# A two-layer sequence kernel on one core: the second sequence's norm scaling moved from VectorE to ScalarE, and a prefetch hint on TensorE's loop

## The chip, the cores and the metric

The kernel runs on one core of one Trainium2 chip. The metric is the device time of one execution in microseconds (us), lower is better. The kernel before was run three times: 1784.64 us is the median, 1784.25 and 1787.32 us are the lowest and the highest.

## What is computed

Sixteen sequences of 256 tokens and 512 features pass through two layers. Only the norms matter for the change:

```python
# layer 0: layer norm with gain and shift from the condition, latent attention with a
# sparse mask (16 heads of 32), then the residual
x = x + attention0(h) @ Wo.T
# layer 1: two RMS norms, each with a gain from the condition
def ada_rms(x, t, w, tw):
    n = x * jax.lax.rsqrt(jnp.mean(jnp.square(x), axis=-1, keepdims=True) + EPS)
    scale = t @ tw.T
    return n * (w * (1.0 + scale))[:, None, :]
h = ada_rms(x, time_emb, ln1_w, ln1_tw)      # into attention 1 (8 query heads of 64)
x = res + ctx @ Wo.T
h = ada_rms(x, time_emb, ln2_w, ln2_tw)      # into the MLP (512 -> 2048 -> 512)
return res + silu(h @ Wg.T) * (h @ Wu.T) @ Wd.T
```

The change touches the multiplication of each row (token) of `x` by its `rsqrt(...)`, in both RMS norms.

## The kernel before, in words

Sequences go in pairs (`s` = 0, 1), so there are 8 pairs. A sequence is two tiles of 128 tokens. All products are made of three f16 matmuls (high times high, high times low, low times high; lines 1436 to 1438), so every operand needs a high and a low half. The high half is made by ScalarE and the low half by VectorE, after it.

The order of the work is written by hand, for each engine apart, and the engines meet by counting semaphores. While pair n is in layers 0 and 1, TensorE also works off the MLP of pair n - 1, cut into 96 parts. `PLAN` (lines 125 to 141) says how many parts stand ahead of each step of pair n. A part is six 128x512 matmuls. The steps around the change are these, with the number of MLP parts ahead of each: `out0b.0` and `out0b.1` (0), `fill2.0` (1), `fill2.1` (1), `kv1.0` (1), `kv1.1` (0) at the end of layer 0; `out1b.0` and `out1b.1` (0), `fill4.0` (2), `fill4.1` (1), `end` (2) at the end of layer 1. The first pair has no MLP beside it.

What happens at such a place, for s = 0 and then s = 1:

- TensorE makes the output projection of the second token tile (`out0b`, `out1b`), and VectorE adds it to the residual (line 1173, into `x_mid`).
- ScalarE squares the row and sums it (`square`, line 1009, whose full output goes unused into `work`). GpSimd makes the root of both tiles' sums (`root`, lines 693 and 696, into `rstd`).
- VectorE scales the rows, `work = x_mid * rstd`, one instruction for each tile (line 1301), and counts each on `work_ready`. It waits for the root of s = 0, scales two tiles, waits for the root of s = 1, scales two tiles.
- TensorE transposes `work` into PSUM (`fill`, line 1463: 8 transposes of 128x128 for a sequence). It waits for `work_ready` tile by tile.
- ScalarE makes the high halves with the gain (line 847, four instructions for a sequence). VectorE makes the low halves (line 1078, four for a sequence), and counts them on `low_made`.
- At the end of layer 0, TensorE then multiplies by the key and value weights (`kv1.0`, `kv1.1`), where `kv1.0` waits for all low halves of s = 0 and `kv1.1` for all of s = 1. At the end of layer 1, the high and low halves go to the next round's MLP (`gate`, `up`), whose first part waits for all of them.

TensorE runs pairs 2 to 7 in one loop of six turns (line 1742, `pe.Fori`). The other engines have loops of their own, which the change leaves as they are.

Of the kernel before, what the change touches and what calls it, by code (L numbers as in the profile page):

```python
# [7 lines left out]
ALU = mybir.AluOpType  # L8
ACT = mybir.ActivationFunctionType
# [8 lines left out]
TILES = TOK // P  # L18
# [23 lines left out]
NP = SEQS // PAIR  # L42
BOTH = range(PAIR)
# [155 lines left out]
def count(n, per, k):  # L199
    i, off = n  # L200
    return off * per + k if i is None else i * per + (off * per + k)


def need(eng, sem, value):
    if isinstance(value, int) and value <= 0:
        return
    eng.wait_ge(sem, value)
# [24 lines left out]
def build(nc, x, cond_t, pos_t, w_ada_t, b_ada_t, wq0_t, wkd_t, wku_t, wvu_t, wo0_t, ln1_w, tw1_t,  # L232
          ln2_w, tw2_t, wq1_t, wk1_t, wv1_t, wo1_t, wg_t, wu_t, wd_t, mask_c, rope0_c, freq_c,
          wgu, out):
    with ExitStack() as ctx:
        def sb(name, shape, dt=F32):
            return ctx.enter_context(nc.sbuf_tensor(name, shape, dt))

        def sem(name):
            return ctx.enter_context(nc.semaphore(name))  # L240

        def sems(name):
            return [sem(f"{name}{s}") for s in BOTH]
# [20 lines left out]
        x_mid = sb("x_mid", [P, PAIR, TILES, D])  # L264
        x_res = sb("x_res", [P, PAIR, TILES, D])
        work = sb("work", [P, PAIR, TILES, D])
# [36 lines left out]
        ln_rstd, rstd = sb("ln_rstd", [P, PAIR, TILES]), sb("rstd", [P, PAIR, TILES])  # L303
# [13 lines left out]
        def bank(name):  # L317
# [63 lines left out]
        square_sum, eps_added, rstd_ready = (  # L381
            sem("square_sum"), sem("eps_added"), sem("rstd_ready"))
        work_ready, hi_done, low_made, norm_high = (
            sem("work_ready"), sem("hi_done"), sem("low_made"), sem("norm_high"))
        full, lat_low, near_low, terms_made, prob_split = (
            sem("full"), sem("lat_low"), sem("near_low"), sem("terms_made"), sem("prob_split"))
        prob_in = [sem(f"prob_in{m}") for m in range(TURNED)]
# [443 lines left out]
        def _(act):  # L831
# [18 lines left out]
            def heads(n, layer, s, t):  # L850
                use = USE[f"heads{layer}", s, t]
                need(act, full, count(n, USES, use + 1))
                act.activation(act_t[s][0][:, :, t * P:(t + 1) * P],
                               work_bank[use % BANKS][:].rearrange("p (c q) -> p c q", c=CH),
                               ACT.Copy).then_inc(hi_done, 1)
# [140 lines left out]
            def finish(n, layer, idle):  # L996
                idle(f"out{layer}a.0", f"out{layer}a.1")
                for s in BOTH:
                    square(n, layer, s, 0)
                idle(f"heads{layer}.0", f"heads{layer}.1")  # L1000
                for s in BOTH:
                    heads(n, layer, s, 1)
                idle(f"out{layer}b.0", f"out{layer}b.1")
                for s in BOTH:
                    square(n, layer, s, 1)

            def square(n, layer, s, t):
                need(act, mid_ready, count(n, 8, 4 * layer + 2 * t + s + 1))
                act.activation(work[:, s, t, :], x_mid[:, s, t, :], ACT.Square,  # L1009
                               accum_out=squares[:, s, t:t + 1]).then_inc(square_sum, 1)  # L1010
# [50 lines left out]
        def _(dve):  # L1061
# [224 lines left out]
            def finish(n, m, layer):  # L1286
                between(m, f"out{layer}a.0", f"out{layer}a.1")
                for s in BOTH:
                    add(n, layer, s, 0)
                for s in BOTH:  # L1290
                    normalise(n, layer, s, 1)
                between(m, f"heads{layer}.0", f"heads{layer}.1")
                for s in BOTH:
                    heads_low(n, layer, s, 1)
                between(m, f"out{layer}b.0", f"out{layer}b.1")
                for s in BOTH:
                    add(n, layer, s, 1)
                for s in BOTH:
                    need(dve, rstd_ready, count(n, 4, 2 * layer + s + 1))
                    for t in range(TILES):  # L1300
                        dve.tensor_scalar(work[:, s, t, :], x_mid[:, s, t, :], rstd[:, s, t:t + 1],
                                          None, ALU.mult).then_inc(work_ready, 1)

            def layer1(n, m):
                for s in BOTH:
# [128 lines left out]
        def _(pe):  # L1434
# [18 lines left out]
            def fill(n, f, s):  # L1453
                for b in range(2):
                    bank_ = bank_for(n, f"fill{f}", s, b)
                    for t in range(TILES):
                        if b == 0 and f == 0:
                            need(pe, ln_ready, count(n, 4, 2 * s + t + 1))
                        elif b == 0:
                            need(pe, work_ready, count(n, 8, 2 * (f - 2) + 2 * s + t + 1))  # L1460
                        src = work[:, s, t] if f else normed[s][:, t]
                        for c in (2 * b, 2 * b + 1):
                            ins = pe.transpose(bank_[:, (c % 2) * TOK + t * P:][:, 0:P],  # L1463
                                               src[:, c * P:(c + 1) * P], ident[:])
                    ins.then_inc(full, 1)
# [273 lines left out]
            layer1((None, 0), None)  # L1739
            layer0((None, 1), (None, 0))  # L1740
            layer1((None, 1), (None, 0))
            with pe.Fori(0, NP - 2) as i:
                layer0((i, 2), (i, 1))
                layer1((i, 2), (i, 1))
            for part in range(PARTS):
# [70 lines left out]
```

## Time and profile before

| What | Value |
|---|---|
| Median of 3 runs | 1784.64 us (1784.25 to 1787.32) |
| The profiled execution's own time | 1784.77 us |
| Its span, first to last instruction | 1782.8 us |
| TensorE busy | 1711.2 us, 96% |
| VectorE busy | 1158.1 us, 65% |
| ScalarE busy | 944.4 us, 53% |
| GpSimd busy | 399.0 us, 22% |
| Mean granted TensorE clock | 0.977 |

The page of the profile gives busy time by engine over the whole span. In it PE is TensorE's matmuls, PEld its weight loads, DVE VectorE, ACT ScalarE, POOL GpSimd and SP SyncE; L1301 is line 1301 of the kernel. In the timeline, a row is one instruction or a run of the same ones; a bracket at its end tells how long the engine was idle before it and what released it. The ends of matmuls are modelled, so the distance from start to start tells more than the duration.

### The profile page before, as it was taken

What the parts mean: (1) busy time and instruction counts of PE and PEld (TensorE: products, weight loads), DVE (VectorE), ACT (ScalarE), POOL (GpSimd) and SP (SyncE); (2) the same over time, 40 slices, a digit from 0 to 9 for tenths busy, and PEclk for the clock granted to TensorE, in tenths of its full rate; (3) what the DMA queues carried; (4) which work ended last, traced back from release to release, by engine and by line L of the source; (5) the groups of instructions that cost most, each with busy time, mean ns of one, the idle gap of its engine ahead of it and who ended that gap; (6) DMA issues with size and microseconds to landing.
All of it is one profiled execution on the core that took longest, in us unless ns stands there. A gap on an engine that the chain in (4) does not pass through costs nothing.

```text
span 1782.8 us, 37773 instructions
## 1 busy us (share of the span) xinstructions
PE 1711.2 (96%) x12440; PEld 932.5 (52%) x12440; DVE 1158.1 (65%) x2858; ACT 944.4 (53%) x2769; POOL 399.0 (22%) x556
## 2 busy tenths in 40 slices
PE   6676999999999999999999999999999999999999
PEld 2344545555455555555455655555555554555444
DVE  6759666675767667685676766676676856767320
ACT  3836456354664538564583546655484645835320
POOL 3438587011111112111110111111111111102120
PEclk9776999999999999999999999999999999999999
DMA  7866499462785349572693637754486716936320
GB/s 246 152 188 113 128 218 255 94 109 84 173 168 96 82 120 198 122 123 75 145 195 86 112 93 169 163 104 93 110 198 115 133 63 148 199 89 102 102 70 24
DMA packets 527231, 234.30 MB, mean 131 GB/s; under 512 B 476336, under 2 KB 493744, under 8 KB 527024
## 3 DMA queue, kind: packets, MB, share of 16 engines
q1 hardware_dynamic: 511472, 175.09, 49.3%
q10 hardware_dynamic: 15552, 56.63, 10.3%
q8 instruction: 108, 1.77, 0.4%
q14 instruction: 99, 0.81, 0.2%
HBM read 90.09 MB, written 16.78 MB: 60 GB/s over the span
## 4 chain that ended last, share of the span: by engine, by line
PE 78%; DMA 3%; DVE 2%; issue 2%; SPq 1%; ACT 1%; POOL 0%; DVEq 0%; ACTq 0%
PE up L1436 8%; PE up L1437 8%; PE up L1438 8%; PE gate L1436 8%; PE gate L1438 8%; PE gate L1437 8%; PE y L1438 4%; PE y L1437 4%; PE y L1436 4%; PE bank L1436 3%; PE bank L1437 3%; PE bank L1438 3%; PE bank L1463 2%; DMA prob_t<-prob 2%; PE bank L1507 2%
## 5 line engine op out<-in xcount | busy, mean ns | idle before, releaser
L864 ACT ACTIVATE bank<-bank,low 128x128 f32<-128x128 f32 (+2 forms) x768 | 301.9, 394 | 69.1 <-DVE low L1106 36.2
L702 POOL TENSOR_TENSOR inner_t<-inner,inner_t 128x512 f16<-128x512 f32 x128 | 150.7, 1177 | 641.6 <-ACT inner_t L1045 641.5
L1113 DVE TENSOR_TENSOR prob<-bank,prob 128x512 f16<-128x512 f32 (+1 forms) x320 | 202.7, 634 | 49.1 <-ACT prob L873 48.0
L873 ACT ACTIVATE prob<-bank 128x512 f16<-128x512 f32 (+1 forms) x320 | 178.2, 557 | 64.5 <-DMA prob_t<-prob 37.1
L1391 DVE SCALAR_TENSOR_TENSOR silu<-silu,gate 128x512 f32<-128x512 f32 x128 | 87.8, 686 | 170.7 <-ACT silu L1039 169.9
L1436 PE MATMUL gate<-mlp,ring 128*128 128x512 f16 x512 | 193.9, 379 | 1.7 <-DVE silu L1391 1.4
L1436 PE MATMUL up<-mlp,ring 128*128 128x512 f16 x512 | 193.8, 379 | 0.3 <-DVE inner L1401 0.3
L1438 PE MATMUL gate<-mlp,ring 128*128 128x512 f16 x512 | 194.0, 379 | 0.0
L1437 PE MATMUL gate<-mlp,ring 128*128 128x512 f16 x512 | 193.9, 379 | 0.0
L1438 PE MATMUL up<-mlp,ring 128*128 128x512 f16 x512 | 193.9, 379 | 0.0
L1437 PE MATMUL up<-mlp,ring 128*128 128x512 f16 x512 | 193.9, 379 | 0.0
L864 ACT ACTIVATION_READ_ACCUMULATOR bank<-bank,low 128x1 f32 x768 | 156.4, 204 | 0.0
L1039 ACT ACTIVATE silu<-gate 128x512 f32<-128x512 f32 x128 | 76.4, 597 | 127.9 <-PE gate L1438 127.5
L1102 DVE CUSTOM_DVE_ANT_0 bank<-bank,mask 128x128 f32<-128x128 f32 (+1 forms) x448 | 133.3, 351 | 1.9 <-PE bank L1507 1.9
L1009 ACT ACTIVATE work<-x_mid 128x512 f32<-128x512 f32 x64 | 40.3, 630 | 170.7 <-DVE x_mid L1173 170.7
L1045 ACT ACTIVATE inner_t<-inner 128x512 f16<-128x512 f32 x128 | 80.7, 630 | 92.8 <-DVE inner L1401 91.8
L1401 DVE SCALAR_TENSOR_TENSOR inner<-up,silu 128x512 f32<-128x512 f32 x128 | 88.3, 689 | 56.1 <-PE up L1438 46.7
L1436 PE MATMUL y<-v_hi,prob_t 128*128 128x32 f16 (+2 forms) x1024 | 110.0, 185 | 1.3 <-DVE work L1161 0.6
L1437 PE MATMUL y<-v_lo,prob_t 128*128 128x32 f16 (+2 forms) x1024 | 109.0, 184 | 0.0
L1438 PE MATMUL y<-v_hi,prob_t 128*128 128x32 f16 (+2 forms) x1024 | 108.9, 184 | 0.0
L1436 PE MATMUL bank<-wo_hi,act_hi 128*128 128x512 f16 x256 | 98.3, 384 | 1.3 <-DVE act_lo L1087 1.3
L1438 PE MATMUL bank<-wo_hi,act_lo 128*128 128x512 f16 x256 | 98.3, 384 | 0.0
(182 smaller groups left out, 4045.7 us busy)
## 6 DMA issues: line engine op xcount, KB each, us to landing
ring<-wgu_dram ACTq DMA_DIRECT2D x108, 512.0 KB, 3.8
x_in<-x_dram SPq DMA_DIRECT2D x18, 512.0 KB, 3.8
x_res<-x_mid SPq DMA_DIRECT2D x16, 512.0 KB, 3.0
wgu_dram<-ring SPq DMA_DIRECT2D x16, 512.0 KB, 3.6
out_dram<-x_res SPq DMA_DIRECT2D x32, 256.0 KB, 2.3
prob_t<-prob SPq DMA_TRANSPOSE x256, 3.5
inner_t<-wd_t_dram SPq DMA_DIRECT2D x4, 1024.0 KB, 8.9
ring<-wg_t_dram SPq DMA_DIRECT2D x16, 256.0 KB, 4.0
```

The costliest lines, as they stand in the source:

```text
L702: pool.tensor_tensor(inner_t[:, 1, f, :], inner[:], inner_t[:, 0, f, :], ALU.subtract).then_inc(inner_low, 1)
L864: ins = act.activation(bank_[:, at:at + wid], bank_[:, at:at + wid], ACT.Exp, bias=low[:, j % BANKS, k:k + 1], scale=-1.0, accum_out=total)
L873: act.activation(terms(prob[:, g % SLOTS, 0, :], layer, j), terms(work_bank[USE[f"unit{layer}", j] % BANKS][:], layer, j), ACT.Copy).then_ ...
L1039: act.activation(silu[:], gbank[:], ACT.Tanh, scale=0.5 / WS).then_inc(tanh_done, 1)
L1045: act.activation(inner_t[:, 0, f, :], inner[:], ACT.Copy).then_inc(inner_high, 1)
L1102: ins = dve.tensor_tensor_reduce(out=view, in0=view, in1=mask[:, 0:wid], scale=1.0, scalar=3.0e38, op0=ALU.add, op1=ALU.min, accum_out=low ...
L1113: dve.tensor_tensor(terms(prob[:, slot, 1, :], layer, j), terms(work_bank[USE[name] % BANKS][:], layer, j), terms(prob[:, slot, 0, :], lay ...
L1391: dve.scalar_tensor_tensor(silu[:], silu[:], 1.0, gbank[:], ALU.add, ALU.mult).then_inc(gated, 1)
L1401: dve.scalar_tensor_tensor(inner[:], ubank[:], 0.5 * HS / (WS * WS), silu[:], ALU.mult, ALU.mult).then_inc(inner_ready, 1)
L1436: pe.matmul(out_ap, left[0], right[0], start=start, stop=False)
L1437: pe.matmul(out_ap, left[0], right[1], start=False, stop=False)
L1438: return pe.matmul(out_ap, left[1], right[0], start=False, stop=stop)
```

## The change

The two tiles of s = 1 are scaled by ScalarE, as an activation Copy with a per-row scale, directly behind its squares. VectorE keeps s = 0. The semaphore `work_ready` becomes one for each sequence. TensorE's loop is opened with `hint_back_edge=True`.

```diff
-            sem("work_ready"), sem("hi_done"), sem("low_made"), sem("norm_high"))
+            sems("work_ready"), sem("hi_done"), sem("low_made"), sem("norm_high"))
...
                 idle(f"out{layer}b.0", f"out{layer}b.1")
                 for s in BOTH:
                     square(n, layer, s, 1)
+                need(act, rstd_ready, count(n, 4, 2 * layer + 2))
+                for t in range(TILES):
+                    act.activation(work[:, 1, t, :], x_mid[:, 1, t, :], ACT.Copy,
+                                   scale=rstd[:, 1, t:t + 1]).then_inc(work_ready[1], 1)
...
                     add(n, layer, s, 1)
-                for s in BOTH:
-                    need(dve, rstd_ready, count(n, 4, 2 * layer + s + 1))
-                    for t in range(TILES):
-                        dve.tensor_scalar(work[:, s, t, :], x_mid[:, s, t, :], rstd[:, s, t:t + 1],
-                                          None, ALU.mult).then_inc(work_ready, 1)
+                need(dve, rstd_ready, count(n, 4, 2 * layer + 1))
+                for t in range(TILES):
+                    dve.tensor_scalar(work[:, 0, t, :], x_mid[:, 0, t, :], rstd[:, 0, t:t + 1],
+                                      None, ALU.mult).then_inc(work_ready[0], 1)
...
                         elif b == 0:
-                            need(pe, work_ready, count(n, 8, 2 * (f - 2) + 2 * s + t + 1))
+                            need(pe, work_ready[s], count(n, 4, f - 2 + t + 1))
...
-            with pe.Fori(0, NP - 2) as i:
+            with nc.Fori(0, NP - 2, engines=(pe.engine,), hint_back_edge=True) as i:
```

ScalarE's instructions in its loop, at the end of layer 0, before. The first row is the square of the second token tile of s = 1, the rows of L847 are the high halves of `fill2.0`:

```order
L1009 ACTIVATE work,squares<-x_mid 128x512 [waits mid_ready]
L207 REGISTER_ALU
L847 REGISTER_ALU [waits full]
L847 ACTIVATE act_hi<-bank,gain 128x256
L847 REGISTER_ALU
L847 ACTIVATE act_hi<-bank,gain 128x256
```

The same place after the change:

```order
L1013 ACTIVATE work,squares<-x_mid 128x512 [waits mid_ready]
L207 ISA
L1008 ACTIVATE work<-x_mid,rstd 128x512 [waits rstd_ready]
L1008 ACTIVATE work<-x_mid,rstd 128x512
L207 REGISTER_ALU
L847 REGISTER_ALU [waits full]
L847 ACTIVATE act_hi<-bank,gain 128x256
L847 REGISTER_ALU
L847 ACTIVATE act_hi<-bank,gain 128x256
```

A wait for GpSimd's root of s = 1 and two 128x512 activations now stand ahead of the high halves of s = 0.

TensorE's entry into its loop, after the change. Before, the same rows stand there without the one in the middle that is new:

```order
L1441 MATMUL up<-wd_hi,inner_t 128x512
L1745 UNCONDITIONAL_BRANCH
L1745 BRANCH_PREFETCH_HINT
L1745 ISA
L207 ISA
```

The hint is the first instruction of every turn of the loop; the branch that closes the loop is the same as before.

## Rows read from the trace of the kernel before

**Rows 1.** The page: the span, and busy time of each engine.

```profile
span 1782.8 us, 37773 instructions
PE 1711.2 (96%) x12440; PEld 932.5 (52%) x12440; DVE 1158.1 (65%) x2858; ACT 944.4 (53%) x2769; POOL 399.0 (22%) x556
```

**Rows 2.** Busy time in one round: window, its length, PE, PEld, DVE, ACT, POOL, clock, DMA.

```profile
619.00:827.00 208.00, 206.97 (x1550) 114.27 (x1550) 141.66 (x364) 117.16 (x345) 31.05 (x46) 1.00 0.61 127
```

**Rows 3.** Timeline of POOL, pair 4, end of layer 0: start us, us, instruction.

```profile
955.71 0.69 POOL L696 TENSOR_TENSOR rstd<-shifted,minus_half 128x2 f32<-128x2 f32 x1
```

**Rows 4.** Timeline of DVE, same place, 954 to 961 us.

```profile
954.44 0.87 DVE L1301 TENSOR_SCALAR work<-x_mid,rstd 128x512 f32<-128x512 f32 x2
956.44 0.88 DVE L1301 TENSOR_SCALAR work<-x_mid,rstd 128x512 f32<-128x512 f32 x2 [1.13 <-POOL rstd L696]
957.24 1.66 DVE L1078 SCALAR_TENSOR_TENSOR act_lo<-bank,gain,act_hi 128x256 f16<-128x256 f32 x4
959.07 1.66 DVE L1078 SCALAR_TENSOR_TENSOR act_lo<-bank,gain,act_hi 128x256 f16<-128x256 f32 x4 [0.18 <-ACT act_hi L847]
```

**Rows 5.** Timeline of ACT, same place, 955 to 960 us.

```profile
955.93 1.57 ACT L847 ACTIVATE act_hi<-bank,gain 128x256 f16<-128x256 f32 x4 [0.66 <-PE bank L1463]
958.10 1.57 ACT L847 ACTIVATE act_hi<-bank,gain 128x256 f16<-128x256 f32 x4 [0.60 <-PE bank L1463]
```

**Rows 6.** Timeline of PE, same place: transposes of s=0, s=1, then kv1.0, kv1.1.

```profile
955.06 1.18 PE L1463 MATMUL bank<-ident,work 128*128 128x128 f32 x8
...
957.38 1.04 PE L1463 MATMUL bank<-ident,work 128*128 128x128 f32 x8
...
959.54 0.22 PE L1436 MATMUL bank<-wkv_hi,act_hi 128*128 128x128 f16 x1
...
960.88 0.22 PE L1436 MATMUL bank<-wkv_hi,act_hi 128*128 128x128 f16 x1
```

**Rows 7.** ACT's groups, shapes apart: busy us, mean ns of one, idle before.

```profile
L1009 ACT ACTIVATE work<-x_mid 128x512 f32<-128x512 f32 x64 | 40.3, 630 | 170.7 <-DVE x_mid L1173 170.7
...
L847 ACT ACTIVATE act_hi<-bank,gain 128x256 f16<-128x256 f32 x64 | 25.1, 475 | 10.3 <-PE bank L1463 10.3
...
L940 ACT ACTIVATE lat_hi<-bank 128x256 f16<-128x256 f32 x16 | 6.2, 385 | 28.9 <-PE bank L1438 28.8
```

**Rows 8.** Timeline of ACT: two 128x512 activations from SBUF back to back.

```profile
345.89 1.23 ACT L918 ACTIVATE stack<-work 128x512 f16<-128x512 f32 x2 [4.83 <-DVE work L1203]
```

**Rows 9.** Timeline, pair 4, end of layer 1: the last low halves, the first MLP part.

```profile
1030.91 1.66 DVE L1078 SCALAR_TENSOR_TENSOR mlp<-bank,gain,mlp 128x256 f16<-128x256 f32 x4 [0.50 <-ACT mlp L847]
1034.24 0.38 PE L1436 MATMUL gate<-mlp,ring 128*128 128x512 f16 x1
```

**Rows 10.** Timeline, pair 0: ends of layer 0 (118 us) and layer 1 (193 us).

```profile
118.37 1.58 DVE L1301 TENSOR_SCALAR work<-x_mid,rstd 128x512 f32<-128x512 f32 x2 [1.05 <-POOL rstd L696]
119.87 3.21 DVE L1078 SCALAR_TENSOR_TENSOR act_lo<-bank,gain,act_hi 128x256 f16<-128x256 f32 x8
...
192.92 0.88 DVE L1301 TENSOR_SCALAR work<-x_mid,rstd 128x512 f32<-128x512 f32 x2 [1.06 <-POOL rstd L696]
193.72 3.47 DVE L1078 SCALAR_TENSOR_TENSOR mlp<-bank,gain,mlp 128x256 f16<-128x256 f32 x8
...
197.24 0.39 PE L1436 MATMUL gate<-mlp,ring 128*128 128x512 f16 x1
```

**Rows 11.** The loop line of TensorE: duration in ns, smallest, median, largest.

```profile
L1742 PEldq COMPARE_BRANCH  x6: 83/3498/3826, 614.9 to 1651.9; - x6
```

**Rows 12.** Timeline of PE at the loop's entry, and at one back edge.

```profile
411.33 0.49 PE L1463 MATMUL bank<-ident,stack 128*128 128x128 f32 x3
...
1032.48 0.38 PE L1438 MATMUL up<-wd_hi,inner_t 128*128 128x512 f16 x1
1033.32 0.87 PE L1463 MATMUL bank<-ident,stack 128*128 128x128 f32 x6 [0.46 <-issue]
```

**Rows 13.** Waits of PE, all of the span: us in total, times, longest.

```profile
PE bank L1463 <- issue: 2.9, 5, 0.8
```

## The prediction, made before the changed kernel ran

> **What bounds the kernel now.** I read the page first. TensorE is busy for 1711.2 of the span's 1782.8 us, VectorE for 65%, ScalarE for 53% [rows 1]. A share over the whole span hides stages, so I took the stretches of single rounds next: in the round from 619 to 827 us TensorE is busy for 206.97 of 208 us at full granted clock [rows 2]. In rounds with an MLP beside them the matmuls are back to back. There a change is worth what it adds to or takes from TensorE's own gaps. Work that other engines save is worth nothing. So the question for each part is whether TensorE comes to wait, and where it waits now.
>
> The third view is the timeline of four engines at the end of layer 0 in pair 4, as one example of seven. GpSimd's root of s = 1 ends at 955.71 + 0.69 = 956.40 [rows 3]. VectorE scales s = 0 at 954.44 and, after 1.13 us of idling, s = 1 at 956.44; its low halves of s = 0 start at 957.24 and end at 958.90, those of s = 1 run from 959.07 to 960.73 [rows 4]. ScalarE makes the high halves of s = 0 from 955.93 and those of s = 1 from 958.10 [rows 5]. TensorE transposes s = 0 at 955.06 and s = 1 at 957.38, and starts kv1.0 at 959.54 and kv1.1 at 960.88 [rows 6]. Between these it has MLP parts. The low halves of s = 0 are there 0.64 us before kv1.0 wants them, those of s = 1 only 0.15 us before kv1.1. The transposes of s = 1 don't wait for the scaling that the change moves. This is the finding that decides: the moved step has almost no idle time to win here, and the steps behind it have 0.15 to 0.64 us to lose.
>
> **The scaling on ScalarE.** First its price. The square of a 128x512 tile, from SBUF to SBUF with no per-row operand, takes 0.63 us. A per-row scale makes a 256-wide activation 475 ns long where the one with a constant takes 385 ns [rows 7]. So I take 0.63 + 0.09 = 0.72 us for one scaling. Two 128x512 activations behind each other take 1.23 us, so they start 1.23 - 0.63 = 0.60 us apart [rows 8]. VectorE took 0.48 us for one and 0.88 us for both [rows 4].
>
> By order the two scalings now stand ahead of ScalarE's high halves of s = 0, together with the wait for the root of s = 1. Queued behind that wait are all eight activations of both sequences, and behind them VectorE's low halves and kv1. In pair 4:
>
> - The wait ends at 956.44, as VectorE's did. The scalings start at 956.44 and 957.04, and the next instruction can start at 957.64. The high halves of s = 0 start at 957.64 and not at 955.93: 1.71 us later.
> - They start (1.57 - 0.47)/3 = 0.37 us apart [rows 5]. The second ends at 957.64 + 0.37 + 0.47 = 958.48. VectorE follows such an end by 0.13 us (958.10 + 0.37 + 0.47 = 958.94 against 959.07, [rows 4, 5]). Its four low halves run from 958.61 to 960.27. Before, they ended at 958.90.
> - TensorE wants them at 959.54 and sees them at about 960.37, taking 0.1 us for the way. kv1.0 starts 0.83 us late.
> - The low halves of s = 1 follow at once, from 960.18 to 961.84. kv1.1 would start at 960.37 + 1.34 = 961.71 and starts at 961.94: another 0.23 us. Together 1.06 us.
> - The second tile of s = 1 is scaled at 957.76. The transposes want it at 957.60, and wait for 0.16 to 0.2 us. This delay is not added, since kv1.0 waits longer anyway.
> - VectorE's 0.88 us that go away are worth nothing: it idled before them, and would idle in their place.
>
> Pairs 1 to 7 have the same steps and the same number of parts: 7 x 1.06 = 7.4 us.
>
> Pair 0 has no MLP beside it. ScalarE is free for the high halves 1.20 us after 118.37, the low halves start 0.37 + 0.47 + 0.13 us later, at 120.54, and eight of them end 3.2 us after that, at 123.8 instead of 123.08 [rows 10]: 0.7 us. At the end of layer 1 the same sum from 192.92 gives a start at 195.09 instead of 193.72 and an end at about 198.3. The first MLP part stood right behind that end at 197.24 [rows 10]: 1.1 us.
>
> The ends of layer 1 in the other pairs I cost at nothing. The last low half is ready at 1030.91 + 1.66 = 1032.57, and the first MLP part starts at 1034.24 [rows 9]. That cover is 1.67 us, more than the 1.1 us of pair 0. Were it gone, each would cost up to 1.1 us.
>
> The scaling part costs 7.4 + 0.7 + 1.1 = 9.2 us. Its lower end: with the square's own 0.63 us and starts 0.53 us apart (an activation without any overhead of the per-row operand), the high halves come 0.14 us earlier, and each pair loses 0.9 us, in all 7.8 us. The upper end: with scalings that don't overlap (0.72 us apart) each loses 1.3 us, in all 10.8 us. I take 9.2, since the 1.23 us pair of rows 8 is the nearest row. One semaphore for each sequence costs and gives nothing: TensorE waits for the same events in the same order.
>
> Here a rule speaks against the change. The trace shows VectorE at 0.48 us for a tile and an activation of that size at 0.63 us [rows 4, 7], with VectorE busy for 65% [rows 1]. The Trainium skill (Perfetto Trace Analysis, Optimizing Scalar/DVE Operations) says that an operation that VectorE runs in one of its faster modes is quicker there, and that moving it to ScalarE may make sense where VectorE is saturated. By that rule alone the price would be the difference of the two tiles, 2 x 0.24 = 0.5 us for each place, about half of mine, since the rule doesn't see the queue behind the step.
>
> **The loop hint.** TensorE's loop branch takes 3.5 to 3.8 us when it is taken, five times, and 0.08 us the last time, when it isn't [rows 11]. TensorE's queue of matmuls covers most of it: at 1032.48 the last matmul of a turn starts, 0.22 us of work, and the next starts at 1033.32. That is 0.84 - 0.22 = 0.62 us of gap, where the entry into the loop at 411.33, with the same instructions behind it, has none [rows 12]. The five gaps are 2.9 us in the view of waits [rows 13]. That view counts from the modelled end of a matmul, 0.16 us after its successor could have started (0.38 against 0.22 us), so the true sum is 2.9 + 5 x 0.16 = 3.7 us. With the target fetched ahead, the branch should be short and the gaps go. I take all 3.7 us. The bounds are a hint that does nothing (0) and one that takes all (3.7). The other side, a loss, can only be the one added instruction in each turn, and the queue covers it unless the branch is still long.
>
> **Sum.** 1784.8 us of the profiled execution + 9.2 - 3.7 = 1790.3 us. The median of the runs stands 0.1 us lower, so 1790.1 us, 0.3% slower. What counts as a difference is 0.2%, 3.6 us here, about what a measurement can tell from no change.
>
> **Rivals.**
>
> A. The hint doesn't shorten the branch. For it: no row shows a hinted branch. Against it: the taken branch is 3.5 us and the other 0.08, so the price is that of reaching the target. Time: 1784.6 + 9.2 = 1793.8 us. The Trainium skill (Runtime: NRT & Kernel Launch, Instruction fetch mechanics) says that fetch ahead is purely sequential and that a taken branch out of its window has to fetch first; it knows no hint, and by it alone this rival would hold. The 3.5 us agree with it, the hint is untested here.
>
> B. Faster: the late low halves don't reach TensorE. This needs the shift of the low halves of s = 0 to stay under the 0.64 us of cover instead of 1.37 us, in the place of kv1.0 [rows 4, 6], for instance if ScalarE ran the high halves of s = 0 while it waits. Then only the hint counts: 1784.6 - 3.7 = 1780.9 us. Against it stands the order of ScalarE's queue.
>
> C. Within 0.2%: the place costs half of what I work out, by the difference of durations alone or since later gaps of TensorE shrink when it comes late. 16 scaled tiles in the ends of layer 0 at 0.24 us are 3.8 us, against 3.7 us from the hint: 1784.7 us. Against it: in a round TensorE has 1.03 us of gaps in all [rows 2], and those wait for chains that start with TensorE and move with it.
>
> **How the numbers follow.** My case 0.62, with its own range 1788.5 to 1792.5 (7.8 to 10.8 us against 3.7, and a part of the hint missing). A 0.16, C 0.12, B 0.08. The last 0.02 is something slower that I don't see. Slower by over 0.2%: 0.62 + 0.16 + 0.02 = 0.80. Same: 0.12. Faster: 0.08. The range takes in my case and A, and C's upper part: 1785.0 to 1794.3 us.
>
> **What would show it.** In the changed profile: kv1.0 and kv1.1 with a wait for VectorE's low halves (0.2 to 0.9 us each in seven pairs), ScalarE's first high half of layer 0 about 1.7 us later against the root of s = 1, two activations of 0.7 us in front of it, no wait at the first MLP part but in pair 0. The loop branch well under 1 us, and no gap at the back edges. A kv1.0 that starts without a wait would prove me wrong, and so would a branch of 3.5 us or a time under 1788 us.

## The result, and the profile after

| | before | changed |
|---|---|---|
| Median | 1784.78 us (1782.82 to 1788.01, 14 runs) | 1790.23 us (1787.91 to 1795.45, 14 runs) |
| Changed / before, 95% interval | | 1.0034 [1.0026, 1.0041] |
| Span of the profiled execution | 1782.8 us | 1788.1 us |

The change makes the kernel 5.4 us slower by the medians, where 5.5 us were forecast; by the ratio it is 6.1 us (4.6 to 7.3). The runs below show that the number is better than its working: the two parts that were priced came out nearly as worked out, and two things that were not in the sum, of about 3 us each, had opposite signs.

The page of the changed kernel, as in [rows 1]:

```profile
span 1788.1 us, 37791 instructions
PE 1716.8 (96%) x12440; PEld 934.4 (52%) x12440; DVE 1144.4 (64%) x2826; ACT 963.0 (54%) x2801; POOL 398.9 (22%) x556
```

32 instructions went from VectorE (2858 to 2826) to ScalarE (2769 to 2801). VectorE has 14 us less to do, ScalarE 19 us more, and neither number tells what happened to the time.

The view of instruction groups has the price of one scaling, 714 ns, and who released the idle time ahead of it:

```profile
L1008 ACT ACTIVATE work<-x_mid,rstd 128x512 f32<-128x512 f32 x32 | 21.4, 714 | 18.3 <-POOL rstd L696 18.3
```

The prediction took 0.72 us. It stands on the difference between 475 and 385 ns in [rows 7]. The Trainium skill (ScalarE: Activation LUTs, What ACT_TABLE_LOAD costs) gives some 93 ns for each per-row operand; 714 - 630 = 84 ns agrees.

**The end of layer 0 in pair 4**, the place of [rows 3 to 6], 5 us later in the run. Timeline of the changed kernel; start us, us, instruction, in brackets idle time before it and its releaser:

```profile
960.44 0.69 POOL L696 TENSOR_TENSOR rstd<-shifted,minus_half 128x2 f32<-128x2 f32 x1
...
961.16 1.33 ACT L1008 ACTIVATE work<-x_mid,rstd 128x512 f32<-128x512 f32 x2 [1.16 <-POOL rstd L696]
...
962.10 1.32 PE L1466 MATMUL bank<-ident,work 128*128 128x128 f32 x8
...
962.40 3.00 ACT L847 ACTIVATE act_hi<-bank,gain 128x256 f16<-128x256 f32 x8
...
963.38 3.23 DVE L1082 SCALAR_TENSOR_TENSOR act_lo<-bank,gain,act_hi 128x256 f16<-128x256 f32 x8 [3.34 <-ACT act_hi L847]
...
965.17 0.23 PE L1439 MATMUL bank<-wkv_hi,act_hi 128*128 128x128 f16 x1 [0.45 <-DVE act_lo L1082]
```

ScalarE waits for the root, scales two tiles, and comes to the high halves 1.24 us after the scalings began (1.20 forecast). High halves and low halves, two separate groups of four each before, have grown into runs of eight without a break. VectorE is idle for 3.34 us before the low halves: the 0.88 us taken from it turned into idling. And kv1.0, which found everything ready before [rows 6], now waits. From start to start, TensorE loses 0.61 us at kv1.0, 0.15 at kv1.1 and 0.23 between the transposes of the two tiles of s = 1, in all 0.99 us (1.06 forecast, of another split: 0.83 and 0.23).

The view of waits puts the same down to these lines (line waited for, us, times, longest):

```profile
PE bank L1439 <- DVE act_lo L1082: 4.0, 8, 0.9
...
PE bank L1466 <- DVE work L1304: 2.5, 2, 1.3
PE bank L1466 <- ACT work L1008: 2.0, 2, 1.0
```

Before, the same view has for the low halves and for the scaled rows

```profile
PE bank L1463 <- DVE work L1301: 4.7, 5, 1.3
...
PE bank L1436 <- DVE act_lo L1078: 0.7, 1, 0.7
```

So kv1 waited once before, in pair 0, and waits in all eight pairs now. For the transposes this view shows no more than before (2.5 + 2.0 against 4.7 us), since their new waits are too short for it. It counts from modelled ends of matmuls. By starts, the waits at kv1 are 5.3 us and those inside the transposes rose from 1.1 to 3.0 us, over the rounds behind pair 0. Together that is 7.2 us, where the sum had 7.4.

**The end of layer 1**, same pair, the place of [rows 9]:

```profile
1035.37 3.23 DVE L1082 SCALAR_TENSOR_TENSOR mlp<-bank,gain,mlp 128x256 f16<-128x256 f32 x8 [3.31 <-ACT mlp L847]
...
1039.47 0.38 PE L1439 MATMUL gate<-mlp,ring 128*128 128x512 f16 x1
```

The low halves end at 1038.60, 0.87 us before the first MLP part, which has no wait. The cover of 1.67 us in the prediction held.

**Pair 0**, the place of [rows 10]. kv1.0 waits for the low halves of layer 0, and at the end of layer 1 the first MLP part waits for those of the MLP's input:

```profile
121.38 3.23 DVE L1082 SCALAR_TENSOR_TENSOR act_lo<-bank,gain,act_hi 128x256 f16<-128x256 f32 x8 [3.15 <-ACT act_hi L847]
...
123.14 0.26 PE L1439 MATMUL bank<-wkv_hi,act_hi 128*128 128x128 f16 x1 [0.92 <-DVE act_lo L1082]
...
199.35 3.23 DVE L1082 SCALAR_TENSOR_TENSOR mlp<-bank,gain,mlp 128x256 f16<-128x256 f32 x8 [3.15 <-ACT mlp L847]
...
202.64 0.39 PE L1439 MATMUL gate<-mlp,ring 128*128 128x512 f16 x1 [0.56 <-DVE mlp L1082]
```

By starts the two places lose 0.65 and 1.05 us (0.7 and 1.1 forecast). But the first transposes of pair 1 start at 200.33 and not at 195.19 us, 5.1 us late, and only 1.7 us of it are these places. Some 0.8 us are of the start of the execution, ahead of the changed work. The rest, 2.6 us, is a difference and not a row. Most of it is clock: matmul by matmul, the lag behind the kernel before grows by 0.7 us around 176 us and by 1.7 us from 188.1 to 191.5 us, both at a lower clock than before. Busy time in two stretches of 10 and 4 us: window, length, PE, PEld, DVE, ACT, POOL, granted clock, DMA share, GB/s:

```profile
170.00:180.00 10.00, 8.91 (x88) 6.63 (x86) 7.88 (x15) 7.72 (x24) 9.67 (x15) 0.61 0.78 150
...
188.00:192.00 4.00, 4.00 (x13) 1.47 (x11) 0.35 (x1) 0.00 (x0) 0.00 (x0) 0.57 0.00 0
```

The same views of before:

```profile
170.00:180.00 10.00, 9.36 (x104) 6.50 (x105) 7.08 (x12) 6.63 (x20) 9.43 (x16) 0.84 0.92 136
...
185.00:190.00 5.00, 5.00 (x24) 2.25 (x24) 1.38 (x2) 0.72 (x2) 0.60 (x2) 1.00 0.06 25
```

In a stretch in which TensorE is busy all the time, it is granted 0.57 of the clock and not 1.00, and starts 13 matmuls in 4 us. In its timeline the distance changes from 0.216 us (2.4 GHz) to 0.43 us (1.2 GHz) with the same instruction, 128x512:

```profile
187.66 0.38 PE L1439 MATMUL bank<-wo_hi,act_hi 128*128 128x512 f16 x1 [0.67 <-DVE act_lo L1091]
187.88 0.40 PE L1440 MATMUL bank<-wo_lo,act_hi 128*128 128x512 f16 x1
188.09 0.61 PE L1441 MATMUL bank<-wo_hi,act_lo 128*128 128x512 f16 x1
188.50 0.63 PE L1439 MATMUL bank<-wo_hi,act_hi 128*128 128x512 f16 x1
188.93 0.63 PE L1440 MATMUL bank<-wo_lo,act_hi 128*128 128x512 f16 x1
```

**The loop branch**, to be held against [rows 11] and [rows 12]: its instructions (times, ns min/median/max), and the matmuls on both sides of the back edge that the prediction took as its example.

```profile
L1745 PEldq BRANCH_PREFETCH_HINT  x6: 36/36/45, 413.6 to 1450.2; - x6
...
L1745 PEldq COMPARE_BRANCH  x6: 88/352/389, 620.8 to 1656.9; - x6
```

```profile
1038.38 0.38 PE L1441 MATMUL up<-wd_hi,inner_t 128*128 128x512 f16 x1
1038.59 0.60 PE L1466 MATMUL bank<-ident,stack 128*128 128x128 f32 x4
```

3.5 us have become 0.35 us, the hint costs 0.04 us, and from start to start the edge takes 0.21 us where it took 0.84. The gap at an edge is that distance less the 0.22 us of the matmul, 0.62 us here. The five gaps that are gone were 0.84 + 0.64 + 0.62 + 0.96 + 0.65 = 3.7 us.

**What doesn't fit.** 7.2 + 1.7 - 3.7 = 5.2 us, and 2.6 us of low clock are to be added, with 0.8 us at the start. The spans differ by 5.3 us only. What comes back is in layer 1 of the later rounds. All other gaps of TensorE in the rounds of pairs 2 to 7 (those over 0.1 us, from start to start) sum to 3.06 us before and to 0.27 us now; over all rounds behind pair 0 the fall is 3.5 us. They are mostly transposes that wait for probabilities. The view of waits of before had

```profile
PE bank L1471 <- DVE prob L1113: 4.9, 8, 1.7
```

and that of the changed kernel has

```profile
PE bank L1474 <- DVE prob L1117: 1.8, 3, 0.8
```

This was rival C's second argument, that later gaps shrink when the place comes late. So the experiments had to price each part by itself, and to tell whether the 3.5 us come back because TensorE is late.

### The profile page after: what moved, and what is told of

Same layout as the page of the kernel before. It is cut to its first block, busy times and chain, and to the rows that moved or that the text cites. A ratio compares the mean times of both kernels' runs of the same rounds, so it can differ in the third digit from the quotient of the medians.

```text
span 1788.1 us, 37791 instructions
## 1 busy us (share of the span) xinstructions
PE 1716.8 (96%) x12440; PEld 934.4 (52%) x12440; DVE 1144.4 (64%) x2826; ACT 963.0 (54%) x2801; POOL 398.9 (22%) x556
## 4 chain that ended last, share of the span: by engine, by line
PE 80%; DMA 2%; DVE 1%; issue 1%; ACT 1%; POOL 0%; SPq 0%; DVEq 0%; ACTq 0%; POOLq 0%
PE up L1439 9%; PE up L1440 9%; PE up L1441 9%; PE gate L1439 8%; PE gate L1440 8%; PE gate L1441 8%; PE y L1441 4%; PE y L1440 4%; PE y L1439 4%; PE bank L1439 4%; PE bank L1441 4%; PE bank L1440 4%; DMA prob_t<-prob 2%; PE bank L1510 2%; PE bank L1474 1%; PE bank L1466 1%
## 5 line engine op out<-in xcount | busy, mean ns | idle before, releaser
L1440 PE MATMUL bank<-wo_lo,act_hi 128*128 128x512 f16 x256 | 99.2, 387 | 0.0
```

Of the source, the lines that this page charges most:

```text
L1440: pe.matmul(out_ap, left[0], right[1], start=False, stop=False)
```

## The experiments

Two theories are set against each other in the expectations. One is the sum of the prediction: the price of a place is set by what is queued behind the two scalings, whatever comes later. The other is that about half of a delay comes back in TensorE's later gaps. A ratio is that of an experiment to the kernel before, run on the same chip, with its 95% interval; 0.001 is 1.8 us.

### The two parts of the change

**e1_hint_only** is the kernel before with this one edit; **e2_scale_only** is the changed kernel with it undone.

```diff
-            with pe.Fori(0, NP - 2) as i:
+            with nc.Fori(0, NP - 2, engines=(pe.engine,), hint_back_edge=True) as i:
```

> The kernel before with the loop hint alone; VectorE scales both sequences. Theory Q (the prediction's sum: each scaling on ScalarE delays the queue behind it, the hint takes the five gaps at the back edges): -3.7 us against before, about 1781.0 us; the branch near 0.35 us, no gap at the back edges. Rival M (the parts don't add: TensorE's gaps later in layer 1 grow or shrink by about as much, since they hang on DMA transposes that collide with other transfers): anything from -1 to -6 us, with the gaps in layer 1 of a different size than before.

> The whole change without the hint. Theory Q: +9.2 us against before, about 1793.9 us, and about 3.7 us more than the changed kernel. Rival C (the place costs the difference of durations only, or half of it comes back later): +4 to +5 us, about 1789 us, no different from the changed kernel.

e1: 0.9986 [0.9978, 0.9995], -2.5 us (-3.9 to -0.9). e2: 1.0062 [1.0050, 1.0074], +11.0 us (8.9 to 13.2). The branch in e1:

```profile
L1742 PEldq COMPARE_BRANCH  x6: 88/352/389, 615.5 to 1649.5; - x6
```

The hint works alone as it does with the scalings, and rival A is out. The scalings were worked out at 9.2 us, with an upper end of 10.8, and measured at 11.0: a fifth more, though the interval takes in 9.2. In e2's profile the waits at kv1 are 5.3 us and the transposes' 2.9 us, as in the changed kernel, and pair 0 ends 3.7 us late, with its low clock. The two parts alone add up to 11.0 - 2.5 = 8.5 us, where together they cost 6.1 us (1.0034 of 1785). The 2.4 us between them are within the three intervals, so the medians don't show that anything isn't additive.

### The two layers

```diff
+                if layer == 0:
                     need(act, rstd_ready, count(n, 4, 2 * layer + 2))
...
                                       None, ALU.mult).then_inc(work_ready[0], 1)
+                if not (layer == 0):
+                    need(dve, rstd_ready, count(n, 4, 2 * layer + 2))
+                    for t in range(TILES):
+                        dve.tensor_scalar(work[:, 1, t, :], x_mid[:, 1, t, :], rstd[:, 1, t:t + 1],
+                                          None, ALU.mult).then_inc(work_ready[1], 1)
```

ScalarE's two scalings stand under the first condition, and in the other layer VectorE scales s = 1 as before. This is **e3_layer0_only**; **e4_layer1_only** has `layer == 1`, and **e11_layer1_again** is e4 once more, on another chip.

> The change with ScalarE's scaling in the ends of layer 0 alone; at the ends of layer 1 VectorE scales both sequences. Theory Q: 7 x 1.06 + 0.7 - 3.7 = +4.4 us against before, about 1789.1 us. A rival in which the cost sits in pair 0 (a lower clock there after longer waits) expects near -2 us, about 1782 us.

> The change with ScalarE's scaling in the ends of layer 1 alone; at the ends of layer 0 VectorE scales both. Theory Q: the low halves have 1.67 us of cover there, so only pair 0 pays: +1.1 - 3.7 = -2.6 us against before, about 1782.1 us. The rival in which any ScalarE scaling costs the same expects 4.6 - 3.7 = +1 us, about 1785.7 us.

e3: 1.0030 [1.0019, 1.0042], +5.4 us (3.4 to 7.5). e4: 0.9977 [0.9968, 0.9986], -4.1 us. The whole loss is in layer 0. In layer 1 the same two activations, with the same 0.7 us and the same wait ahead of the same high halves, cost only pair 0's 1.05 us, which e4's profile shows at the same place as [rows 10]. The difference is the cover of 1.67 us. e4 is the fastest kernel of the study, faster than before and than the changed one (for e1 the intervals overlap).

> The version with the hint and ScalarE's scaling in the ends of layer 1 alone once more, beside the one with the hint alone in a neighbour's place. Theory Q: 1.1 us more than the hint alone, about -2.6 us against before. If its -4.1 us of the first time holds, it is the best version.

e11: 0.9975 [0.9966, 0.9984], -4.5 us. Both times e4's edit is some 2 us below e1 (0.0009 and 0.0011, where each interval reaches 0.0009 to either side), though its sum should be 1.1 us above it. What that means is with e12 below.

### Pair 0

```diff
+                if not at_start(n):
                     need(act, rstd_ready, count(n, 4, 2 * layer + 2))
...
+                if not (not at_start(n)):
+                    need(dve, rstd_ready, count(n, 4, 2 * layer + 2))
```

> The whole change, but in pair 0 VectorE scales both sequences in both layers. Theory Q: 7 x 1.06 - 3.7 = +3.7 us against before, about 1788.4 us, 1.8 us less than the changed kernel. Rival P (in pair 0 the change costs near 5 us, as the profiled execution of the changed kernel shows by the start of pair 1, a part of it as a stretch at the lower clock): about 0 to +1 us, near 1785 us.

**e5_not_pair0** leaves pair 0 as it was: 1.0012 [1.0003, 1.0021], +2.2 us (0.5 to 3.7). Against the changed kernel's 1.0034 pair 0 is worth 0.0022, 3.9 us, twice the 1.8 us of the sum, with an uncertainty of some 2 us from the two intervals. In e5's profile pair 0 ends at 195.29 us (before: 195.19), and the stretch ahead of pair 0's last output projection has its clock back:

```profile
184.00:189.00 5.00, 4.33 (x22) 2.10 (x23) 2.08 (x3) 1.21 (x3) 0.83 (x3) 1.00 0.00 0
```

The row of e3, which has the scalings in pair 0's layer 0, reads

```profile
184.00:189.00 5.00, 4.19 (x13) 1.72 (x14) 1.38 (x2) 1.16 (x2) 0.31 (x1) 0.67 0.00 0
```

13 matmuls started and not 22. The stretch of 3.4 us at the 1.2 GHz level is in the profiles of the changed kernel, e2, e3, e7 and e8, all with ScalarE scaling in pair 0's layer 0, and not in those of before, e1, e4, e5, e9, e11 and e12, where VectorE does it. e6, below, is the exception: ScalarE scales there, later in its queue, and the stretch isn't there. Its low clock comes later: from 193 to 200 us it has 0.51, where the kernel before has 0.76:

```profile
193.00:200.00 7.00, 6.13 (x23) 4.01 (x24) 3.30 (x9) 6.18 (x12) 1.24 (x4) 0.51 0.93 272
...
193.00:200.00 7.00, 6.31 (x29) 4.33 (x30) 5.12 (x12) 6.31 (x14) 1.64 (x5) 0.76 1.03 314
```

Each of these is one profiled execution, and pair 0 has low stretches in every one of them, that of before too. They also move without any change of the work. e12, below, has e4's pair 0, instruction for instruction, and reaches pair 1 at 192.5 us where e4 and e11 take 195.9 and 195.8. From 150 to 160 us the clocks of e12 and e4 were

```profile
150.00:160.00 10.00, 6.32 (x84) 5.21 (x85) 10.00 (x18) 7.66 (x25) 6.86 (x13) 0.83 0.66 126
...
150.00:160.00 10.00, 7.99 (x80) 6.26 (x80) 10.00 (x21) 8.29 (x28) 4.67 (x9) 0.50 0.77 147
```

So a low stretch at this place goes with the delay in five profiles of six, but one execution can be 3.4 us off by its clock alone. That the delay causes the stretch is likely and not shown.

### The place in ScalarE's queue

**e6_behind_highs** moves the two scalings behind the high halves of s = 0:

```diff
                     fill(n, 2, s)
                     behind(f"fill2.{s}")
+                    if s == 0:
+                        scale(n, 0)
```

and the same at `fill4`, with nothing behind the squares.

> The changed kernel with ScalarE's two scalings behind the high halves of s = 0 instead of ahead of them, in both layers. If only the queue behind the scalings counted, this would cure it: about 1782 us, like the hint alone. Theory Q looks at what TensorE wants next: the transposes of s = 1 then wait 0.9 us for the first tile and 0.3 us for the second, at both layers' ends, where the ends of layer 1 cost nothing before: 14 x 1.2 + 2.5 - 3.7 = +15.6 us against before, about 1800 us, with no wait for low halves at kv1.

e6: 1.0067 [1.0051, 1.0084], +12.0 us (9.1 to 15.0), in four executions. The sum's 15.6 us is outside that. The profiled one, the slowest of the four, has a span 15.8 us longer than before, and by starts its transposes wait 17.1 us more behind pair 0 (14 x 1.2 = 16.8 expected). The wait changed its line. All 16 places wait for ScalarE's scaling now, and kv1 for nothing:

```profile
PE bank L1472 <- ACT work L1003: 13.7, 16, 2.0
```

This order isn't the cure: the high halves of s = 0 are early, and the transposes of s = 1 [rows 6], which come next on TensorE, are late instead. They had even less time to lose than kv1.

**e8_first_on_act** gives ScalarE s = 0, whose root is there earlier, and VectorE s = 1:

```diff
-                for s in BOTH:
-                    square(n, layer, s, 1)
+                square(n, layer, 0, 1)
+                need(act, rstd_ready, count(n, 4, 2 * layer + 1))
+                for t in range(TILES):
+                    act.activation(work[:, 0, t, :], x_mid[:, 0, t, :], ACT.Copy,
+                                   scale=rstd[:, 0, t:t + 1]).then_inc(work_ready[0], 1)
+                square(n, layer, 1, 1)
```

> The other sequence moved: ScalarE scales s = 0, between its squares of s = 0 and of s = 1, where it idles 1.87 us for VectorE; VectorE scales s = 1. Hint kept. Theory Q: TensorE's wait of 0.28 us at the transposes of s = 0 goes, the squares and the root of s = 1 come 0.5 us later, and kv1.0 about 0.3 us later with no wait for low halves; the ends of layer 1 cost nothing: 7 x 0.3 - 3.7 = -1.6 us against before, about 1783.3 us. The rival in which a scaling on ScalarE costs about 1 us wherever it stands expects about 1789 us.

e8: 0.9992 [0.9980, 1.0004], -1.4 us (-3.6 to +0.7). That is 0.0042, 7.5 us, under the changed kernel, with the same number of tiles on the same engines. At kv1 nothing waits that didn't before. The price isn't there, as was expected, but at the transposes of s = 1, which wait for VectorE nine times, six of them from pair 2 on:

```profile
PE bank L1466 <- DVE work L1304: 4.5, 9, 1.8
```

By starts all transposes behind pair 0 wait 2.4 us more than before, against 7.2 us at the transposes and kv1 in the changed kernel. Against the hint alone (0.9986) the scalings cost 0.0006 here and 0.0048 in the changed kernel, by which of the two sequences ScalarE takes.

**e7_one_more** puts a third scaling in front of the two, with a wait on a semaphore of its own. Its result is written over:

```diff
                 need(act, rstd_ready, count(n, 4, 2 * layer + 2))
+                act.activation(work[:, 1, 1, :], x_mid[:, 1, 1, :], ACT.Copy,
+                               scale=rstd[:, 1, 1:2]).then_inc(extra, 1)
+                need(act, extra, count(n, 2, layer + 1))
                 for t in range(TILES):
```

> The changed kernel with one more 128x512 scaling on ScalarE ahead of the two (its result is written over), 0.8 us with the wait for it. Theory Q: kv1 comes 0.8 us later in each of seven pairs and both ends of pair 0 as well: +7.2 us against the changed kernel, about 1797.5 us. Rival M (about half comes back in TensorE's later gaps): +3.5 us, about 1794 us. A rival in which the cost of the change lies elsewhere than in this queue: no difference.

e7: 1.0087 [1.0055, 1.0119], +15.5 us (9.8 to 21.3), 9.5 us above the changed kernel, where the sum said 7.2 and half of it would be 3.6. With four executions, one at 1811.01 us, the time alone doesn't tell the two apart. The trace does: by starts the transposes of the seven later pairs wait 5.5 us more than in the changed kernel, 0.78 us each and the whole of the added delay, and the span is 9.7 us longer. Its waits:

```profile
PE bank L1469 <- ACT work L1011: 7.1, 9, 1.7
PE bank L1442 <- DVE act_lo L1085: 4.0, 8, 0.9
```

The wait at kv1 is 4.0 us as without the third scaling. The new delay is taken at the transposes of s = 1, which are ahead of it: each delay is paid once, where it is met first.

### Does a late TensorE shrink later gaps?

**e10_dve_delay** has VectorE do everything, as before, with the hint, but lets it scale s = 1 of layer 0 twice. This makes TensorE late without any work on ScalarE:

```diff
                     need(dve, rstd_ready, count(n, 4, 2 * layer + s + 1))
+                    if layer == 0 and s == 1:
+                        for t in range(TILES):
+                            dve.tensor_scalar(work[:, s, t, :], x_mid[:, s, t, :],
+                                              rstd[:, s, t:t + 1], None, ALU.mult).then_inc(extra, 1)
+                        need(dve, extra, count(n, 2, 2))
```

> The kernel with the hint alone, where VectorE scales the second sequence at the end of layer 0 twice: a delay of 0.95 us at the same place, with ScalarE left as before. Theory Q: the transposes of s = 1 come 0.6 to 0.7 us later in seven pairs and 0.95 us in pair 0, +5.5 us against the hint alone, +2 us against before. Rival M (a late TensorE gets about half back in its later gaps of layer 1): +3 us against the hint alone, and the other gaps of rounds 2 to 7 fall from 3.8 us to under 2 us. If pair 0 gets its stretch of low clock near 188 us here too, the clock follows the delay and not ScalarE.

e10: 1.0028 [1.0020, 1.0037], +5.0 us (3.6 to 6.6) over before, 7.5 over e1's ratio. Its later gaps didn't shrink: 4.4 us in the rounds of pairs 2 to 7, where e1 has 3.8 us. With e7, this is against the theory that half comes back. Pair 0 lost 3.1 us and not the 0.95 that the doubled scaling accounts for. Here too the clock is lower, in another stretch:

```profile
170.00:180.00 10.00, 8.48 (x79) 6.46 (x80) 7.44 (x13) 6.86 (x23) 9.59 (x15) 0.52 0.79 146
184.00:189.00 5.00, 3.11 (x38) 2.06 (x37) 3.67 (x7) 1.92 (x4) 1.55 (x4) 1.00 0.00 0
```

0.52 from 170 to 180 us, where before had 0.84. So work on ScalarE isn't needed for a lower clock in this pair.

### Where TensorE's loop code lies

If the later gaps don't follow the lateness, they may follow something else that each of these edits moves. **e9_slot** is e1 with another place for the head of TensorE's loop in the instruction stream, and no other difference but one more branch of TensorE at the loop's entry:

```diff
-            with nc.Fori(0, NP - 2, engines=(pe.engine,), hint_back_edge=True) as i:
+            with nc.Fori(0, NP - 2, engines=(pe.engine,), hint_back_edge=True,
+                         head_slot={pe.engine: 64}) as i:
```

**e12_layer1_slot** is e4 with `head_slot={pe.engine: 192}`.

> The kernel with the hint alone, and TensorE's loop body placed at another offset in its code blocks (same instructions, other places where its code is fetched). Theory Q: no difference from the hint alone, about -3 us against before. Rival L (TensorE's gaps in layer 1 depend on where code fetches fall among the DMA transposes of the probabilities): the gaps of rounds 2 to 7 outside of norms and back edges, 3.8 us with the hint alone, change by 1 us or more either way, and the time with them.

> The version with the hint and ScalarE's scaling in layer 1 alone, with TensorE's loop body at a third offset in its code blocks and nothing else changed. Theory Q without L: no difference from that version, -4 us against before. Rival L (where code fetches fall among the DMA transposes sets TensorE's later gaps; it moved the hint alone by 5.5 us): a different time by 1 us or more, and other gaps of rounds 2 to 7 that differ from its 2 us.

e9: 1.0017 [1.0008, 1.0027], against e1's 0.9986: 5.5 us for the same work in the same order. e12: 0.9999 [0.9988, 1.0010], against 0.9977 and 0.9975: 4 us (2 to 3 us by the medians, 1783.43 us against 1785.28). (The partners ran on other chips, each against the kernel before there; e4's edit repeated across two chips to 0.0002.) Neither profiled execution is typical: e12's is its fastest, 5 us under its median, with the clock in pair 0 shown above, and e9's is its slowest, 5.3 us over. So the traces show where the time goes, and not how much of it in a typical execution. In e12 the other gaps of TensorE are 3.9 us in the rounds of pairs 2 to 7, against 1.5 in e4 and 1.9 in e11, as rival L expected. In e9 they are 14.3 us, against 3.8 in e1. In the view of the tile `prob_t` from 400 to 1700 us, the transposes by DMA that bring the probabilities have in e1

```profile
  ACT prob L873: 25.4, 38
...
DMA to landing us min/median/max: 3.0/3.5/6.3
```

and in e9

```profile
  ACT prob L873: 56.9, 50
...
DMA to landing us min/median/max: 3.1/4.1/7.3
```

The first row is how long ScalarE waits for a transpose to be done with its source, the second the time from issue to landing. Before has 19.8 us and a median of 3.6, the changed kernel 18.1 us and 3.5. With the code at e9's place the transposes of this execution were slower. A wait for one of them in e9, and what the queues moved in that time (queue, packets, MB, share):

```profile
1146.43 0.44 PE L1471 MATMUL bank<-ident,work 128*128 128x128 f32 x2 [2.29 <-DVE prob L1113]
```

```profile
q8 instruction: 1, 0.02, 0.7%
...
prob_t<-prob SPq DMA_TRANSPOSE x4, 5.6
```

The same place in e1, where no such wait is:

```profile
q8 instruction: 1, 0.02, 0.6%
...
prob_t<-prob SPq DMA_TRANSPOSE x4, 3.8
```

So one packet of instructions falls there in both. That it is there can't be the whole difference.

Packet by packet, a fetch of instructions (queue q8 or q14) falls into the time of a DMA transpose more often when that is slow: in the kernel before, of the 320 DMA transposes of the whole run (line 582), 133 took over 3.8 us, and 109 of these had such a packet in their time; of the 187 faster ones 38 had one. The changed kernel has 100 of 126 and 52 of 194, e9 119 of 141 and 46 of 179. A transpose that takes longer also has more time to meet a packet, so part of this is bound to be, and e1 has 133 slow ones too, hardly fewer than e9. Shown is that the place of the code alone moves the time by 4 to 5.5 us (by the ratios), and that in e9 this goes through slower transposes. That the fetches themselves slow them is not isolated: no run took the fetches away.

## Why the prediction was right, point by point

- **TensorE's gaps bound the kernel.** Right. VectorE's 14 us less bought nothing, ScalarE's 19 us more cost only what it put in front of others.
- **The scaling in pairs 1 to 7, 7 x 1.06 = 7.4 us.** Right: 7.2 us by starts. The start of the high halves and the price of an activation (0.714 against 0.72 us) were right to 0.04 us. In the split I left out the 0.2 us between the transposes since kv1.0 would wait longer anyway. It was paid there, and kv1.0 and kv1.1 paid less for it.
- **Pair 0, 0.7 + 1.1 us.** Right at the two places (0.65 and 1.05), and wrong as a sum for the pair. The step that failed is that nothing else would happen in it. The delay was followed by a lower granted clock, 2.6 us in the trace; e5 puts the whole of pair 0 at 3.9 us by its ratio. That the delay caused the lower clock is not shown, since it also moves by itself (e12).
- **Ends of layer 1 at nothing.** Right: e4, e11, and the missing wait at 1039.47 us.
- **The rule of VectorE's faster mode.** VectorE's 0.48 us against 0.71 us is as the Trainium skill (Perfetto Trace Analysis, Optimizing Scalar/DVE Operations) has it, and 0.5 us for a place would be half of what the trace shows. In layer 1 it would be too much, in layer 0 too little: what is queued behind the step decides, which a difference of durations can't tell.
- **The hint, -3.7 us.** Right: exactly that at the five back edges. e1's median shows 2.5 us (0.9 to 3.9), with its other gaps 0.8 us larger than before.
- **Rival C, that later gaps shrink.** It was dismissed since these gaps move with TensorE. They did fall, by 3.5 us, in the changed kernel, so the dismissal was wrong. But C's reason is wrong too: e7 and e10 make TensorE later and pay in full, and in the rounds of pairs 2 to 7 the sum is 3.8, 1.5, 1.9 and 14.3 us in e1, e4, e11 and e9, where TensorE isn't late in layer 0 at all. This term was missing from the sum, and by chance it was about as large as the clock's. What sets it is open. The place of the code moves it (e9, e12). So does something that isn't the work of these rounds: e5 does the same in them as the changed kernel, and has 2.3 us where that has 0.3. Over all profiles it is 0.3 to 2.3 us where ScalarE takes scalings (3.9 in e12) and 3.1 us or more where it doesn't, and no run tells whether VectorE's lighter load has a part in that.

So the direction was right for the reason given, each price that was read from rows held to 0.1 us a place, and the agreement of the total to 0.1 us is luck: +2.6 and -3.5 us were missing, and 0.8 us at the start of the one profiled execution. The range of 1785.0 to 1794.3 was about what these two terms need.

## What to carry to other kernels

Before work is moved to the engine with less to do, read what is queued behind the new place, and how long TensorE can do without it: the same two activations cost 1 us a time where the cover was 0.64 us and nothing where it was 1.67 us. Where a saved time of some 0.2% decides, run the candidate with its code at a second place too, since that alone moved this kernel by 0.2 to 0.3%. And hint the back edge of a long loop: here it is one line, and with the scaling moved in layer 1 alone it gives the lowest times of the study, 0.9977 and 0.9975 of before, though at another place of the code the same kernel is at 0.9999.

## What the runs showed of the hardware

- A hinted back edge of TensorE takes 0.35 us and not 3.5, for a hint of 0.04 us. Of the unhinted 3.5 us only 0.6 to 1 us were ever seen by the matmuls, by the queue ahead of them. The Trainium skill (Runtime: NRT & Kernel Launch, Instruction fetch mechanics) says that a branch out of the window has to fetch its target. The trace agrees for the unhinted one of TensorE, at 3.5 us, and e1 shows the hint as the way around it.
- The same section of the Trainium skill (Runtime: NRT & Kernel Launch, Instruction fetch mechanics) calls the cost of passing from one block of code to the next mostly hidden. In these runs the place of TensorE's loop code moved the time by 4 to 5.5 us of 1785 (e1 and e9, e4 and e12). What part of it the fetches have is open.
- In the pair without an MLP beside it, a delay of 0.65 to 1 us in layer 0 was followed by stretches at the lower clock level, in which a TensorE that was busy all the time took 0.43 us for a matmul and not 0.216. By the start of pair 1 some 2.1 to 2.6 us were lost beyond the delays themselves (in the changed kernel, e2, e3 and e10), one execution each. Before it fell at 188 us in the changed kernel, TensorE had been busy for 8.12 of the 10 us from 178 to 188, at full clock; in the kernel before it was for 8.29 of the 10 us from 176 to 186, and the clock stayed. e6 has its low stretch from 193 us on instead, and in e12 this pair is done 3.4 us earlier with no change in it, by its clock, so how far the delay is the cause stays open.
